# Decoder attention on one core: heads paired by halves, exponentials kept in PSUM, loads reordered, all probabilities scaled by ScalarE

## The reference

```python
def attn(h, Wq, Wk, Wv, Wo):                 # h: 2 x 512 x 1024, normalised rows of x
    q = heads(h @ Wq, 32); k = heads(h @ Wk, 8); v = heads(h @ Wv, 8)
    q = q * cos + rotate_half(q) * sin       # rotate_half: [-x2, x1], halves of 64
    k = k * cos + rotate_half(k) * sin
    p = softmax(causal(q @ k.T / sqrt(128)))
    return (p @ repeat(v, 4)) @ Wo
x = x + attn(layernorm(x), Wq, Wk, Wv, Wo)
x = x + fake_quant(layernorm(x)) @ fake_quant(ctx)
x = x + experts(layernorm(x))
```

## Time and profile before

| quantity | value |
|---|---|
| median of 3 executions | 1509.59 us (1508.82 to 1513.8) |
| profiled execution | 1504.89 us, its span 1503.1 us |
| mean granted TensorE clock | 0.954 |
| busy: PE, DVE, ACT, POOL | 1321.1, 1036.4, 703.4, 614.8 us |
| stage of the heads | 190 to 960 us |
| 48 output steps | 960 to 1317 us |

### The profile page before, as it was taken

How to read it: one execution, slowest core, us unless ns; L and a number is a source line. 1 busy time by engine, 2 the same in 40 slices (tenths; PEclk the granted TensorE clock), 3 DMA queues, 4 the chain that set the end, 5 groups by cost and what they waited for, 6 DMA issues and landing times. The chain is left out here.

```text
span 1503.1 us, 20047 instructions
## 1 busy us (share of the span) xinstructions
PE 1321.1 (88%) x7016; PEld 1120.5 (75%) x7025; DVE 1036.4 (69%) x2061; ACT 703.4 (47%) x1395; POOL 614.8 (41%) x454
## 2 busy tenths in 40 slices
PE   5989998989899989999898887969999666788998
PEld 4879996777777878788777776858887554556777
DVE  7785257887777888888888864637675326577863
ACT  4412264555555656566556575623333223355440
POOL 5776765665666666767567442200000000020100
PEclk9999998999999999999999988989999778898999
DMA  6033264257356392745657578784223342300011
GB/s 238 21 117 115 78 190 147 94 155 228 113 139 226 113 292 94 193 123 148 174 148 173 177 254 264 217 227 151 95 96 113 135 157 99 99 3 3 27 42 44
DMA packets 132996, 207.44 MB, mean 138 GB/s; under 512 B 9616, under 2 KB 66960, under 8 KB 129312
## 3 DMA queue, kind: packets, MB, share of 16 engines
q1 hardware_dynamic: 128864, 176.79, 35.3%
q0 software_dynamic: 4032, 29.36, 10.0%
HBM read 147.40 MB, written 88.08 MB: 157 GB/s over the span
## 5 line engine op out<-in xcount | busy, mean ns | idle before, releaser
L1571 PE MATMUL banks<-ob_hi,oa_hi 128*128 128x512 f32 x384 | 160.1, 417 | 62.6 <-DVE ob_lo L1224 60.1
L1766 POOL TENSOR_TENSOR resid<-resid,colterm 128x1024 f32<-128x1024 f32 x8 | 19.8, 2485 | 441.4 <-ACT colterm L1823 350.6
L1187 DVE TENSOR_TENSOR pT_lo<-banks,pT_hi 128x512 fp32r<-128x512 f32 (+1 forms) x192 | 103.9, 594 | 121.5 <-ACT pT_hi L939 121.3
L946 ACT ACTIVATE prob<-prob,small 128x512 f32<-128x512 f32 (+3 forms) x256 | 141.0, 552 | 51.1 <-DVE small L1196 51.0
L1221 DVE TENSOR_TENSOR oa_lo<-oraw,oa_hi 128x1024 fp32r<-128x1024 f32 x48 | 58.8, 1224 | 150.2 <-ACT oa_hi L925 150.1
L1209 DVE TENSOR_SCALAR prob<-prob,small 128x384 f32<-128x384 f32 (+2 forms) x192 | 159.4, 884 | 2.3
L1529 PE MATMUL banks<-xc,nring_hi_b 128*128 128x512 f32 x448 | 144.9, 405 | 15.9 <-DVE n_turn L1147 13.8
L1571 PE MATMUL banks<-ob_lo,oa_hi 128*128 128x512 f32 x384 | 158.2, 412 | 0.0
L1571 PE MATMUL banks<-ob_hi,oa_lo 128*128 128x512 f32 x384 | 157.2, 409 | 0.0
L925 ACT CAST oa_hi<-oraw 128x1024 fp32r<-128x1024 f32 x48 | 50.3, 1048 | 228.3 <-PE banks L1571 100.7
L939 ACT CAST pT_hi<-banks 128x512 fp32r<-128x512 f32 (+1 forms) x192 | 86.8, 523 | 140.2 <-PE banks L1499 140.2
(11 more groups left out here) (237 smaller groups left out, 3502.0 us busy)
## 6 DMA issues: line engine op xcount, KB each, us to landing
q_raw<-qk_dram SPq DMA_DIRECT2D x64, 256.0 KB, 3.3
o_S<-o_st SPq DMA_DIRECT2D x64, 256.0 KB, 4.4
qk_dram<-q_made SPq DMA_DIRECT2D x64, 256.0 KB, 2.1
w<-in_L_attn_Wo SPq DMA_DIRECT2D x32, 512.0 KB, 6.8
oraw<-o_S SPq DMA_DIRECT2D x32, 512.0 KB, 3.7
nraw<-in_L_attn_Wq SPq DMA_DIRECT2D x56, 256.0 KB, 5.2
o_S<-o_S POOLq DMA_DIRECT2D x12, 1024.0 KB, 13.0
o_S<-o_N POOLq DMA_DIRECT2D x12, 1024.0 KB, 13.9
```

Source lines behind the costliest of these rows:

```text
L946: nc.scalar.activation(prob[:, sl], prob[:, sl], ACT.Exp, bias=shift[:, i:i + 1], scale=-1.0, accum_out=total[:, i:i + 1]).then_inc(exp_do ...
L1187: nc.vector.tensor_tensor(pT[1][:, sl], turned_chunk(turned, mixed, c), as32(pT[0][:, sl]), ALU.subtract).then_inc(pT_lo, 1)
L1571: ins = nc.tensor.matmul(step_bank(m, t), oa[a][:, s % 2, k, t * P:(t + 1) * P], ob[c][:, s % 2, k, :], start=(q == 0 and k == 0 and i == ...
```

## The change

It has five parts. (1) A panel's columns are regrouped so that a job yields the first halves of two heads beside their second halves; the rotation then needs two multiplications over 128 partitions instead of two over 64 and one over 128, and two GpSimd operations per pair of products (P2 with P4, P5 with P3) instead of one per product. The stores of a pair go out as four DMAs of 64 partitions at P4 and at P3, and a panel's weights come in two DMAs instead of four. (2) The three narrower tiles' exponentials are written back to the score banks, and ScalarE scales them from there into `prob`; VectorE's three scalings go. The exponential of the second tile waits for one mask more. (3) SP stores turned heads before it loads the next q. (4) 16 of the 32 output-weight loads, two per unit, are issued early instead of 28, three per unit; the rest come two per step in steps 2 to 9; x comes back in steps 10 to 20; the context is loaded from step 28 on, and `load_ctx(n)` stands at step n + 32 instead of n + 30. (5) The first weight sum is formed in steps 4 to 11 instead of 0 to 7, and three jobs go to units 3, 5, 8, 12 and 16 instead of 4, 8, 12 and 16, one to units 50 and 52 instead of 52.

```diff
-                     for p in ((0, 1, 2) if u in (4, 8, 12, 16) else (0,) if u == 52 else (0, 1))]
+                     for p in ((0, 1, 2) if u in (3, 5, 8, 12, 16) else (0,) if u in (50, 52) else (0, 1))]
-EARLY = 28
+EARLY = 2 * PAIRS
@@ SP, store of turned heads @@
+            sp.wait_ge(turn_made, 2 * e + b + 1)
+            for n, (x, y) in enumerate(((0, 1), (1, 0))):
+                rows = slice(64 * n, 64 * n + 64)
+                sp.dma_start(qk_dram[head + n, b, 64 * x:64 * x + 64], made_half(b, 0)[rows, :]).then_inc(q_kept[b], 16)
+                sp.dma_start(qk_dram[head + n, b, 64 * y:64 * y + 64], made_half(b, 1)[rows, :]).then_inc(q_kept[b], 16)
@@ SP, steps of the output product @@
-            for n in rest[3 * (s - 2):3 * (s - 1)]:
-                load_wo_early(n)
+            if s < 2 + PAIRS:
+                load_wo_early(2 * PAIRS + s - 2)
+                load_wo_early(3 * PAIRS + s - 2)
-            n = s - 4 * PAIRS + 2
-            if n == 0:
+            if s == 4 * PAIRS - 4:
                 sp.wait_ge(o_kept[0], o_count(UNITS - 2))
-            if 0 <= n < 2 * KT:
+                load_ctx(0)
+                load_ctx(1)
+            n = s - 4 * PAIRS
+            if 2 <= n < 2 * KT:
                 load_ctx(n)
@@ GpSimd, rotation @@
-            nc.gpsimd.tensor_tensor(q_made[:, n % 2, :], n_turn[:, 0, :], n_turn[:, 1, :], ALU.add
-                                    ).then_inc(turn_made, 1)
+            if b:
+                nc.gpsimd.tensor_tensor(x, q_made[:, 1, :], x, ALU.subtract)
+                nc.gpsimd.tensor_tensor(y, y, q_made[:, 0, :], ALU.add).then_inc(turn_made, 1)
@@ ScalarE, exponentials and scaling @@
-                act.wait_ge(masked_done, 4 * u + n + 1)
-                nc.scalar.activation(prob[:, sl], prob[:, sl], ACT.Exp, bias=shift[:, i:i + 1], scale=-1.0,
+                act.wait_ge(masked_done, 4 * u + (1, 3, 3, 4)[n])
+                nc.scalar.activation(prob[:, sl] if n == 0 else score_tile(i), prob[:, sl], ACT.Exp,
-            nc.scalar.activation(prob[:, 0:512], prob[:, 0:512], ACT.Identity, scale=inv[:, 3:4]).then_inc(wide_done, 1)
+            nc.scalar.activation(prob[:, 0:512], prob[:, 0:512], ACT.Identity, scale=inv[:, 3:4])
+            act.wait_ge(inv_done, 2 * u + 2)
+            act.wait_ge(exp_done, 4 * u + 4)
+            for i in TILE_ORDER[1:]:
+                sl = slice(PROB_AT[i], PROB_AT[i] + P * (i + 1))
+                ins = nc.scalar.activation(prob[:, sl], score_tile(i), ACT.Identity, scale=inv[:, i:i + 1])
+            ins.then_inc(wide_done, 1)
@@ VectorE, rotation and scaling @@
-            nc.vector.tensor_tensor(n_turn[0:64, 0, :], b[64:128, :], sin[64:128, :], ALU.mult)
-            nc.vector.tensor_tensor(n_turn[64:128, 0, :], b[0:64, :], sin[0:64, :], ALU.mult)
-            nc.vector.tensor_tensor(n_turn[:, 1, :], b, cos[:], ALU.mult).then_inc(job_read, 1)
+        def job_turned(b, with_sin, with_cos):
+            nc.vector.tensor_tensor(with_sin, b, sin[:], ALU.mult)
+            nc.vector.tensor_tensor(with_cos, b, cos[:], ALU.mult).then_inc(job_read, 1)
@@ VectorE, read of P3 @@
                 dve.wait_ge(job_read, 6 * e + 4)
+                dve.wait_ge(turn_made, 2 * e + 1)
                 link(nc.vector.tensor_tensor(b, b, n_u[:, 0, :], ALU.add))
-                job_turn(b, 4 * e + TURNS[p])
+                job_turned(b, q_made[:, 0, :], q_made[:, 1, :])
@@ VectorE, scaling @@
-            dve.wait_ge(inv_done, 2 * u + 2)
-            for i in TILE_ORDER[1:]:
-                sl = slice(PROB_AT[i], PROB_AT[i] + P * (i + 1))
-                ins = nc.vector.tensor_scalar(prob[:, sl], prob[:, sl], inv[:, i:i + 1], None, ALU.mult)
-            ins.then_inc(prob_done, 1)
@@ VectorE, steps @@
-            if m < 4:
+            if 4 <= s < 4 + PAIRS:
+                wt(0, s - 4)
+            if 1 <= m < 4:
                 wt(m, q)
```

More of the change, by code:

```diff
@@ L259, in attention @@
     kv_raw, q_raw, qh, q_made, prob, pT, small, mask, o_st, kT, vv = heads
-    nraw, nrings, n_u, n_turn, n_ta, n_p1 = narrow
+    nraw, nrings, n_u, n_turn, n_sin, n_ta, n_p1 = narrow
     w00, w11, w10, w01, oa, p1, ob, oraw = outp
@@ L292, in attention @@
     o_kept = [sem(f"o_kept{n}") for n in range(2)]
-    n_in = [[sem(f"n_in{n}{q}") for q in range(4)] for n in range(2)]
+    n_in = [[sem(f"n_in{n}{q}") for q in range(2)] for n in range(2)]
     n_sum, n_hi, n_lo = sem("n_sum"), sem("n_hi"), sem("n_lo")
@@ L382, in narrow_head, with panel_of @@
         return (Wk, head, head) if kind == "k" else (Wq, head, GROUPS + head)
-    def turn_of(kind, head, b):
-        return 4 * NARROW_HEADS.index((kind, head - head % 2)) + TURN_OF[head % 2, b]
+    def panel_of(kind, head):
+        return NARROW_HEADS.index((kind, head - head % 2))
     def steps_of(u):
@@ L397, in n_quarter, with split, made_half @@
     def n_quarter(e, name):
-        return nraw[:, e % 2, QUARTER[name], :]
+        cols = slice(1, 3) if name[1] == "1" else slice(0, 4, 3)
+        return nraw[:, e % 2, int(name[2]), :, cols, :]
+    def split(ap):
+        return ap.rearrange("p (k a c) -> p k a c", k=KH, a=2)
     def n_factor(j):
         p = SEQ[j % 7]
-        return n_ta[:] if p == "P5" else n_quarter(j // 7, FACTOR[p])
-    def turn_needed(u):
-        return turn_of("q", 4 * (u // 8) + u % 4, batch_of(u))
+        return split(n_ta[:]) if p == "P5" else n_quarter(j // 7, FACTOR[p])
+    def made_half(b, i):
+        return (n_u[:, 1, :] if i else n_sin[:]) if b else n_turn[:, i, :]
     def o_place(u):
@@ L484, in load_narrow @@
                 sp.wait_ge(n_lo, 7 * (e - 1))
[L485 to L491 removed]
+            W, head, _ = narrow_head(e)
+            for k in range(2):
+                sp.dma_start(nraw[:, e % 2, k].rearrange("p k a c -> p k (a c)"),
+                             W[k * 512:k * 512 + 512, head * HEAD:(head + 2) * HEAD].rearrange("(k p) c -> p k c", p=P)
+                             ).then_inc(n_in[e % 2][k], 16)
         def keep_turned(j):
@@ L597, in _ @@
         for u in range(1, UNITS):
+            if (u - 1, 0) in JOB_AT:
+                keep_turned(JOB_AT[u - 1, 0])
             if u + 2 < UNITS:
@@ L614, in _ @@
             if u > JOB_UNIT[JOBS - 5]:
-                for n in range(early, min(early + 3, EARLY)):
+                for n in range(early, min(early + 2, EARLY)):
                     load_wo_early(n)
-                early = min(early + 3, EARLY)
+                early = min(early + 2, EARLY)
         keep_out(UNITS - 2)
@@ L712, in narrow_low @@
             pool.wait_ge(n_hi, j + 1)
-            nc.gpsimd.tensor_tensor(n_ring(1, j), n_factor(j), as32(n_ring(0, j)), ALU.subtract).then_inc(n_lo, 1)
+            nc.gpsimd.tensor_tensor(split(n_ring(1, j)), n_factor(j), split(as32(n_ring(0, j))), ALU.subtract
+                                    ).then_inc(n_lo, 1)
             if j % 7 == 0:
@@ L889, in narrow_high @@
             if p in ("P1", "P2", "P4"):
-                act.wait_ge(n_in[e % 2][QUARTER[FACTOR[p]]], 16 * (e // 2 + 1))
+                act.wait_ge(n_in[e % 2][int(FACTOR[p][2])], 16 * (e // 2 + 1))
             else:
                 act.wait_ge(n_sum, 4 * e + SUMS[{"P6": "S2", "P7": "S3", "P5": "S1", "P3": "S4"}[p]])
-            nc.scalar.copy(n_ring(0, j), n_factor(j)).then_inc(n_hi, 1)
+            nc.scalar.copy(split(n_ring(0, j)), n_factor(j)).then_inc(n_hi, 1)
         def keep_job(j):
```

104 lines of the change are left out of this document (49 added, 55 removed).

## The result

The changed kernel takes 1416.55 us (median of 4 runs, 1411.18 to 1417.88), the kernel before 1509.2 us (4 runs, 1508.13 to 1513.8): ratio 0.9374, 95% interval 0.9342 to 0.9406, 92.7 us faster. The forecast was 1406, range 1378 to 1441. The profiled execution took 1417.59 us, its span is 1415.8 us, 87.3 us shorter than before.

What follows compares the result with a forecast made beforehand. TensorE was taken to bound every stage, losing time to waits and a lower clock. Last steps -67, heads -36 and moved loads 0 gave -103 us: 1402 in the profile, 1406 as a median, range 1378 to 1441.

Steps and rivals of the forecast that it cites:

- Context by two steps, -67: Last 16 steps: SP no longer waits for the same step's quantising; -73.3 us, less +6 for a VectorE stall and clock.
- Scalings on ScalarE: Heads: three ScalarE operations per unit take 1.2 us together; TensorE's 14.8 us of waits for scalings become 2.
- Room of ScalarE's chain, 0.9 us: Heads: slack before TensorE waits for the output copy, about 0.9 us in the unit read, none behind P5's read.
- Rotation, 9.8 us of waits to 3: Heads: job reads 0.69 us shorter cut waits outside units of three jobs from 9.8 us to 3.
- Places of jobs, 17.5 us: Heads: five waits behind units of three jobs, set by middle jobs' operation counts, come to 17.5 us against 15.5 before.
- Output copies, 19 us: Heads: TensorE's copy waits, 30.7 us before, become 10 in unit 56, 4 with two weight loads, 5 for the others.
- the 3 us of part 2: Heads: new TensorE waits for the output copy because ScalarE's chain grows by the scalings; 3 us.
- Loads in steps 2 to 9, 0: Output steps 2 to 9: twelve loads enter; bounds -8 and +15 us, gain in front and load behind cancel, 0.
- Stores before q: Heads: q is asked for up to 3 us later but used a unit later, so it costs 0.
- The heads' sum, -27 of idle time and -9 of clock: Heads: TensorE idle 44.5 against 71.8 us, -27; clock loss 23 to 14, -9; together -36 us.
- The total: Whole kernel: -67 - 36 + 0 = -103 us, giving 1402 in the profile and 1406 as a median.
- Half-width stores: Rival, chance 0.05: stores from 64 partitions take up to twice their time, loading the queue and lengthening waits; 1418 us.

Runs made afterwards that it cites:

- b_ctx: The kernel before with only the context's loads moved: two ahead in step 28, load_ctx(n) at step n + 32; 1440.46 us, ratio 0.9558.
- b_scale: The kernel before with only the narrow exponentials put in PSUM and all scalings on ScalarE; 1491.47 us, ratio 0.9893.
- the two a_vec kernels: The changed kernel with VectorE scaling the three narrow tiles, from PSUM (1415.73 us, ratio 0.9401) or from SBUF (1423.8 us, ratio 0.9443).
- q_early28: a_q_first with 28 output-weight loads issued early, three per unit, instead of 16, two per unit; 1406.82 us, ratio 0.9329.
- a_q_first: The changed kernel with SP loading the next q before the store of place 0, except where q needs that store; 1400.28 us, ratio 0.9301.
- q_rows_ahead: a_q_first with the first two pieces of output-product rows asked for before the last pair of turned heads is stored; ratio 0.9275.

## Why the prediction was right, and where it was not

- *Context by two steps, -67*: measured -69.0 in the change (from the cast of step 32 on), 66 alone in b_ctx. The stall came where it was put, at step 43, with 4.4 us (5.8 in b_ctx, 6.65 and 10.01 us from cast to cast); I had booked 6 with the clock.
- *Scalings on ScalarE*: three operations in 1.2 us (1.19 in the timeline), as taken. The waits for scalings went from 14.8 us to none. b_scale prices the part at 15 us. My reason for the stretching, that VectorE works beside GpSimd, is narrowed by the two a_vec kernels and the counts beside them: only out of SBUF. The Trainium skill (SBUF — State Buffer, SBUF: two separate sides) says that VectorE in a two-port mode and GpSimd lock each other out for a whole instruction; by VectorE: DVE Perf Modes (Why PSUM operands drop a tier) an operand in PSUM bars that mode. The traces agree with both: 90 of 90 long scalings from SBUF began while GpSimd ran, and from PSUM they take 340 to 620 ns, whether it runs or not.
- *Room of ScalarE's chain, 0.9 us*: too small for most units. Twice the scalings made 19 new waits, not 55.
- *Rotation, 9.8 us of waits to 3*: one wait of 2.5 us is left outside the units of three. No run shows how much of this the rotation does and how much the scalings that left.
- *Places of jobs, 17.5 us*: the five waits were 4.02, 2.69, 2.70, 4.01 and 3.42 us, 16.8 in sum.
- *Output copies, 19 us*: with the 3 us of part 2 it was 22 against 29.7 us. Unit 56 had 11.4 (10 forecast), and the one with two weight loads ahead 8.4 us (4 forecast). This term was a quarter too low. In q_early28 three loads per unit come out 4 us dearer than two by the ratios, which these runs do not tell from nothing.
- *Loads in steps 2 to 9, 0*: 189.8 us before from step 0 to step 31, 189.3 now.
- *Stores before q, "q is asked for up to 3 us later and used a unit later: 0"*: **this is the step that failed.** q was asked for behind stores that wait for GpSimd, and beside the summing DMAs; ScalarE waited 22.1 us in 4 waits for it, 10.8 at the longest. a_q_first gives back 14.6 us in the heads of the profile, 16 us by the medians and 11 by the ratios. From the first exponential on, the heads came out at -21.9 instead of -36, and with q first at -36.5.
- *The heads' sum, -27 of idle time and -9 of clock*: that -36.5 with q first meets -36 is partly luck. Its idle time fell by 19.9 us, to 52.0 and not 44.5, mostly since the output copies were mis-sized; its busy time fell by 16.6 us, where I had 9 for the clock.
- *The total*: 1416.55 instead of 1406. The profile is short by 15.7 us of the 103 forecast: 5.2 lost in stage 1, which the forecast left as it was, 14.1 too few in the heads, 2.0 more in the last steps, and 1.7 elsewhere. The step above covers what the heads lack; the 5.2 us are a lower clock, whose cause stays open.
- *Half-width stores*: a rival that I gave 0.05. The 128 KB stores landed after 2.4 us, the 256 KB ones before after 2.1. Half the bytes took as long as all of them. That agrees with the Trainium skill (SBUF — State Buffer, Door 1: The DMA port swizzle), but it would look the same if most of a landing were a fixed time, so these rows do not test the rule. The times of b_ctx, b_scale and a_q_first leave no gap of the 12 us that I gave this rival, but no run took the half width away by itself.

a_q_first is faster than both kernels, and q_rows_ahead has the lowest ratio of all, 0.9275, without being told apart from it.

## What to carry to other kernels

Where one queue issues loads and stores in a written order, ask of each wait in it which later load stands behind; here one such line was worth 66 us and another 11 to 16. Where an operation's maximum is many times its median beside another engine's work, look first whether an operand can move to PSUM, and only then give the work to another engine. A job taken from one unit to shorten a wait leaves that unit without cover, so the sum may stay. And before a stage's gain is put down to a change, look whether the stage began at the same time: here 5.2 us had gone ahead of it.
